# Five zero matmuls, first weights in three loads, and first products in the order of their parts, in a one-core transformer-layer kernel

## The reference, cut to what matters

```python
# x: 1024 tokens x 512; S = 128, F = 1248, G = 6
approx_up = x @ up_w.T                       # 512 -> 128
delta     = x @ gate_w.T - local_point       # 512 -> 128
approx    = approx_up @ local_approx_output.T
for idx in range(G):                         # six powers of delta
    dterm  = exp(log|delta| * (idx + 1) - discount_factor[idx])   # with sign, cut for high powers
    approx = approx + (dterm * approx_up) @ fuse_weight[:, :, idx].T
ffn = (silu(x @ ffn_gate_w.T) * (x @ ffn_up_w.T)) @ ffn_down_w.T
x1  = layernorm(x + approx + ffn)
dq1, dq2, dq3 = nf4_quant_dequant(w1, w2, w3)                     # blocks of 64, hidden width 1376
out = layernorm(x1 + (silu(x1 @ dq1.T) * (x1 @ dq2.T)) @ dq3.T)
```

## Time and profile before

| | |
|---|---|
| median of 3 runs | 418.53 us (418.44 to 418.89) |
| the profiled execution, its own time | 419.06 us |
| its span in the profile | 417.2 us |
| PE busy | 408.3 us |
| DVE, POOL, ACT busy | 314.2, 291.3, 263.9 us |
| DMA share, first 31 us | nearly full; below half in most of the rest |

### The profile page before, as it was taken

One profiled execution on the slowest core, in us unless ns is written; L12 is line 12 of the kernel. 1 busy time (PEld: TensorE's weight loads), 2 busy tenths in 40 slices (PEclk: granted clock), 3 DMA queues, 4 the chain that ended last, 5 costly groups with the idle time before them and its releaser, 6 DMA issues.

```text
span 417.2 us, 5429 instructions
## 1 busy us (share of the span) xinstructions
PE 408.3 (98%) x1820; PEld 334.0 (80%) x1820; DVE 314.2 (75%) x371; ACT 263.9 (63%) x356; POOL 291.3 (70%) x230
## 2 busy tenths in 40 slices
PE   8999999999999999999999999999999999999992
PEld 6888888888878888788888888888888878888882
DVE  3629879879887978999969989898999874115025
ACT  5476676686877547557864976879867864332612
POOL 0078998888995499917992668999989984444330
PEclk9999999999999999999999999999999999999997
DMA  8993110000004342003042000000000000000202
GB/s 267 395 409 131 52 38 26 27 25 25 27 25 126 102 147 101 26 0 103 0 176 97 2 0 1 2 0 0 3 0 0 2 0 2 1 2 1 101 2 101
DMA packets 9355, 26.50 MB, mean 64 GB/s; under 512 B 1296, under 2 KB 1552, under 8 KB 8816
## 3 DMA queue, kind: packets, MB, share of 16 engines
q1 hardware_dynamic: 9328, 26.16, 17.8%
HBM read 24.06 MB, written 2.10 MB: 63 GB/s over the span
## 4 chain that ended last, share of the span: by engine, by line
PE 91%; POOL 2%; DVE 2%; DMA 2%; issue 1%; ACT 0%; SPq 0%; POOLq 0%
PE PS L1178 30%; PE PS L1180 30%; PE PS L1179 30%; DMA h<-xT 2%; POOL l_lo L1133 1%; PE PS L1291 1%; PE PS L1281 1%; POOL level L1103 1%; DVE stats L889 1%; DVE R L884 0%; ACT R L659 0%; DVE x_lo L970 0%; ACT x_hi L573 0%; DVE mv L898 0%; SPq L537 0%
## 5 line engine op out<-in xcount | busy, mean ns | idle before, releaser
L1103 POOL TENSOR_SCALAR level<-side 128x1024 f32<-128x1024 int8 (+2 forms) x119 | 130.0, 1092 | 29.3 <-DVE PS L812 12.1
L1178 PE MATMUL PS<-x_hi,w_hi 128*128 128x512 f32 (+1 forms) x352 | 137.6, 391 | 0.2 <-DVE x_lo L970 0.2
L1180 PE MATMUL PS<-x_hi,w_lo 128*128 128x512 f32 (+1 forms) x352 | 137.1, 390 | 0.0
L1179 PE MATMUL PS<-x_lo,w_hi 128*128 128x512 f32 (+1 forms) x352 | 137.0, 389 | 0.0
L812 DVE TENSOR_TENSOR PS<-PS,level 128x1024 f32<-128x1024 f32 (+2 forms) x102 | 120.3, 1179 | 21.5 <-POOL level L1103 16.8
L573 ACT ACTIVATE side<-Q 128x1024 int8<-128x1024 f32 (+1 forms) x77 | 76.5, 1031 | 18.6 <-DVE PS L808 9.7
L1133 POOL TENSOR_TENSOR l_lo<-h,l_hi 128x512 fp32r<-128x512 f32 (+1 forms) x42 | 58.3, 1396 | 38.5 <-ACT l_hi L573 38.0
L1178 PEld LDWEIGHTS PS<-x_hi,w_hi 128*128 128x128 f32 (+1 forms) x352 | 65.2, 185 | 15.0 <-issue 0.6
L1180 PEld LDWEIGHTS PS<-x_hi,w_lo 128*128 128x128 f32 (+1 forms) x352 | 65.2, 185 | 14.9
L1179 PEld LDWEIGHTS PS<-x_lo,w_hi 128*128 128x128 f32 (+1 forms) x352 | 65.2, 185 | 14.5
L1178 PE MATMUL PS<-x_hi,l_hi 128*128 128x512 f32 x144 | 56.7, 394 | 0.0
(11 more groups left out here) (77 smaller groups left out, 500.4 us busy)
## 6 DMA issues: line engine op xcount, KB each, us to landing
Q<-w SPq DMA_DIRECT2D x10, 512.0 KB, 13.8
raw<-w_in SPq DMA_DIRECT2D x9, 512.0 KB, 11.4
raw<-w_out SPq DMA_DIRECT2D x14, 256.0 KB, 2.6
raw<-w SPq DMA_DIRECT2D x2, 1376.0 KB, 8.4
R<-xN SPq DMA_DIRECT2D x2, 1024.0 KB, 5.4
out<-R SPq DMA_DIRECT2D x8, 256.0 KB, 2.0
raw<-w_fuse SPq DMA_DIRECT2D x7, 256.0 KB, 2.5
h<-xT SPq DMA_DIRECT2D x3, 512.0 KB, 7.1
```

The costliest lines, as they stand in the source:

```text
L1103: g.tensor_scalar(level_of(s), side_of(s), LIMITS[k][1], LIMITS[k][0], ALU.min, ALU.max).then_inc(s_level, 1)
L1178: t_.matmul(dst, a_hi, b_hi, start=start, stop=False)
L1179: t_.matmul(dst, a_hi, b_lo, start=False, stop=False)
L1180: return t_.matmul(dst, a_lo, b_hi, start=False, stop=stop)
```

## The change

`WARM` goes from 8 to 5. The weights of pre are loaded in three parts, for chunk 0, for chunk 1, and for chunks 2 and 3, and ACT and DVE split them in those three parts. Chunk 1 of `x` is loaded in two halves, as chunk 0 was. The two small loads `point` and `discount` become one load of 7 columns, `consts` (made on the host with the discounts repeated for each row), which is issued after job 1 and unit 0; job 1 is now ahead of unit 0. On ACT the exponential of the discounts moves behind the split of job 1. For chunk 0 PE takes the matmuls by the part they need: for a half of the tokens first both products of `w_hi` with `x_hi`, then both of `w_lo` with `x_hi`, then both of `w_hi` with `x_lo`, where each of the latter two groups waits for its own part.

```diff
-WARM = 8
+WARM = 5
...
-            sp.dma_start(w_raw(0)[:, 0:PRE0], w_pre[:, 0:PRE0]).then_inc(s_pre_raw, 16)
-            sp.dma_start(xT_raw[:, 0, 0:HALF], xT[:, 0, 0:HALF]).then_inc(s_x[0], 16)
-            sp.dma_start(xT_raw[:, 0, HALF:TOK], xT[:, 0, HALF:TOK]).then_inc(s_x0b, 16)
-            sp.dma_start(w_raw(0)[:, PRE0:1024], w_pre[:, PRE0:1024]).then_inc(s_raw[0], 16)
-            for c in range(1, DC):
+            for c in range(DC):
+                if c < 2:
+                    part = slice(c * PRE0, (c + 1) * PRE0)
+                    sp.dma_start(w_raw(0)[:, part], w_pre[:, part]).then_inc(s_pre_raw[c], 16)
+                    for a in range(2):
+                        ts = slice(a * HALF, (a + 1) * HALF)
+                        sp.dma_start(xT_raw[:, c, ts], xT[:, c, ts]).then_inc((s_x, s_xb)[a][c], 16)
+                    continue
+                if c == 2:
+                    sp.dma_start(w_raw(0)[:, 2 * PRE0:1024], w_pre[:, 2 * PRE0:1024]).then_inc(s_raw[0], 16)
                 sp.dma_start(xT_raw[:, c, :], xT[:, c, :]).then_inc(s_x[c], 16)
-            sp.dma_start(point_sb[:], point).then_inc(s_point, 16)
-            sp.dma_start(disc[:], discount.broadcast_to([P, G])).then_inc(s_point, 16)
+            load_job(1)
             load_unit(0)
-            load_job(1)
+            sp.dma_start(term_consts[:], consts).then_inc(s_point, 16)
             load_unit(1)
...
             act.wait_ge(s_line0, 1)
-            act.wait_ge(s_point, 32)
-            nc.scalar.activation(fact[:], disc[:], ACT.Exp, scale=-1.0).then_inc(s_fact, 1)
             split_raw(1)
+            act.wait_ge(s_point, 16)
+            nc.scalar.activation(fact[:], disc, ACT.Exp, scale=-1.0).then_inc(s_fact, 1)
             act.wait_ge(s_pre, 2)
...
-            for c in range(DC):
-                if c == 0:
-                    pe.wait_ge(s_pre_hi, 1)
-                    pe.wait_ge(s_pre_lo, 1)
-                elif c == 1:
+
+            pe.wait_ge(s_pre_hi, 1)
+            for half in range(2):
+                xs = slice(half * HALF, (half + 1) * HALF)
+                pe.wait_ge(s_xh, half + 1)
+                for kind in (1, 0):
+                    t_.matmul(PS[:, 2 * kind + half, :], wh0[:, kind, 0, :], x_hi[:, 0, xs], start=True, stop=False)
+                pe.wait_ge(s_pre_lo, 1)
+                for kind in (1, 0):
+                    t_.matmul(PS[:, 2 * kind + half, :], wl0[:, kind, 0, :], x_hi[:, 0, xs], start=False, stop=False)
+                pe.wait_ge(s_xl, half + 1)
+                for kind in (1, 0):
+                    t_.matmul(PS[:, 2 * kind + half, :], wh0[:, kind, 0, :], x_lo[:, 0, xs], start=False, stop=False)
+            for c in range(1, DC):
+                if c == 1:
+                    pe.wait_ge(s_pre_hi, 2)
+                    pe.wait_ge(s_pre_lo, 2)
+                elif c == 2:
                     wait_raw(0)
```

More of the change, by code:

```diff
@@ L256, in job_rows, with build @@
     return P if kind == "fuse" else rows(f, F1) if kind == "out" else rows(f, F2)
-def build(nc, xT, xN, w_pre, w_fuse, w_in, w_out, point, discount, w12, w3, ident_in, out):
+def build(nc, xT, xN, w_pre, w_fuse, w_in, w_out, consts, w12, w3, ident_in, out):
     with ExitStack() as ctx:
@@ L278, in build @@
         ident = sb("ident", [P, P])
-        point_sb, disc, fact = sb("point_sb", [P, 1]), sb("disc", [P, G]), sb("fact", [P, G])
+        term_consts, fact = sb("term_consts", [P, 1 + G]), sb("fact", [P, G])
+        point_sb, disc = term_consts[:, 0:1], term_consts[:, 1:1 + G]
         stats, mv = sb("stats", [P, TT, 6]), sb("mv", [P, TT, 2])
@@ L338, in build @@
         s_zero, s_warm = sem("s_zero"), sem("s_warm")
-        s_pre_raw, s_pre_hi, s_pre_lo = sem("s_pre_raw"), sem("s_pre_hi"), sem("s_pre_lo")
+        s_pre_raw, s_pre_hi, s_pre_lo = [sem(f"s_pre_raw{c}") for c in range(2)], sem("s_pre_hi"), sem("s_pre_lo")
         s_point, s_ident = sem("s_point"), sem("s_ident")
         s_x = [sem(f"s_x{c}") for c in range(DC)]
-        s_x0b = sem("s_x0b")
+        s_xb = [sem(f"s_x{c}b") for c in range(2)]
         s_R = [sem(f"s_R{a}") for a in range(2)]
@@ L958, in _ @@
             hi0, lo0 = raw_parts(0)
-            dve.wait_ge(s_pre_hi, 1)
-            v.tensor_tensor(lo0[:, 0:PRE0], w_raw(0)[:, 0:PRE0], hi0[:, 0:PRE0].bitcast(F32),
-                            ALU.subtract).then_inc(s_pre_lo, 1)
             for c in range(DC):
                 for a in range(2):
-                    if c == 1 and a == 0:
+                    if c < 2 and a == 0:
+                        part = slice(c * PRE0, (c + 1) * PRE0)
+                        dve.wait_ge(s_pre_hi, c + 1)
+                        v.tensor_tensor(lo0[:, part], w_raw(0)[:, part], hi0[:, part].bitcast(F32),
+                                        ALU.subtract).then_inc(s_pre_lo, 1)
+                    elif c == 2 and a == 0:
+                        part = slice(2 * PRE0, 1024)
                         dve.wait_ge(s_whi, 1)
-                        v.tensor_tensor(lo0[:, PRE0:1024], w_raw(0)[:, PRE0:1024], hi0[:, PRE0:1024].bitcast(F32),
+                        v.tensor_tensor(lo0[:, part], w_raw(0)[:, part], hi0[:, part].bitcast(F32),
                                         ALU.subtract).then_inc(s_wlo0, 1)
@@ L977, in _ @@
             beside()
-            dve.wait_ge(s_point, 32)
+            dve.wait_ge(s_point, 16)
             dve.wait_ge(s_pre, 1)
-            v.tensor_scalar(delta, PS[:, 2:4, :], point_sb[:, 0:1], None, ALU.subtract).then_inc(s_delta, 1)
+            v.tensor_scalar(delta, PS[:, 2:4, :], point_sb, None, ALU.subtract).then_inc(s_delta, 1)
             for i in range(2 * C1):
@@ L1312, in _ @@
                     last = product(PS[:, 2 * kind + half, :], wh0[:, kind, c, :], wl0[:, kind, c, :],
-                                   x_hi[:, c, xs], x_lo[:, c, xs], c == 0, c == DC - 1)
+                                   x_hi[:, c, xs], x_lo[:, c, xs], False, c == DC - 1)
                     if c == DC - 1 and half == 1:
@@ L1391 @@
         "w_out": np.ascontiguousarray(a(L0_attn_ffn_down_w).T[:, order]),
-        "point": a(L0_attn_local_point).reshape(S, 1),
-        "discount": a(L0_attn_discount_factor).reshape(1, G),
+        "consts": np.concatenate([a(L0_attn_local_point).reshape(S, 1),
+                                  np.broadcast_to(a(L0_attn_discount_factor).reshape(1, G), (S, G))], axis=1),
         "w12": by_squares(a(L0_ffn_w1), a(L0_ffn_w2)),
```

12 lines of the change are left out of this document (7 added, 5 removed).

## The result

| | before | changed |
|---|---|---|
| median of 19 runs each | 418.67 us (418.25 to 419.35) | 417.87 us (417.59 to 418.53) |
| ratio | | 0.9983, 95% interval 0.9976 to 0.9989 |
| profiled execution, its own time | 419.06 us | 418.42 us |
| its span | 417.2 us | 416.5 us |

417.87 lies inside the predicted range of 416.7 to 418.3, and 0.57 above the predicted 417.3. By the ratio the kernel is faster by 0.7 us (0.5 to 1.0), some 0.6 of the 1.26 us forecast. That is a little under the 0.84 us that I had called the least difference to be told, so it stands at the line between "faster" and "within 0.2%"; with 19 runs on each side the interval does exclude no change.

A forecast was written before the change was run, and what follows sets the result against it. PE bounds the kernel, from when it works without a hole, set by chunk 1's load. 0 (halves) - 1.26 + 0 (loads) + 0 (unit 0) takes 419.06 to 417.80; median 0.53 below, 417.3; range 416.7 to 418.3.

The forecast's parts named there:

- What bounds the kernel, and that the gain lasts: PE works without a hole once chunk 1 has landed; POOL's list moves with PE, so the 1.26 us stays.
- The halves of chunk 1: Chunk 1's first half lands near 7.6, not 8.84; PE starts chunk 1 at 9.12, not 10.38: 1.26 us gained.
- That load keeps its place in bytes and lands at 10.16: Chunk 2's load of `x` lands at 10.16, its products can start at 11.7, and PE wants it at 11.88.
- what is late next: Check of the loads behind chunk 1: chunk 2 has 0.2 us to spare, chunk 3 is ready at 13.4 against 14.6.
- 1.51: Time in us from a chunk's landing, through ACT's `x_hi` and DVE's `x_lo`, to PE's first product of it.
- The sum: Gain of 1.26 us off the profiled 419.06 gives 417.80; the median stands 0.53 below that execution, so 417.3.
- The set-up rival: Each added load pays 1.7 us in the queue; chunk 2 lands at 13.56, 1.9 us slower, 420.5; chance 0.05.
- Five zero matmuls: Before chunk 0 on PE: alone gains nothing; without it chunk 0 ends at 10.03, giving back 0.91 us.
- Order by parts: Chunk 0's second half on PE starts at 7.33 and ends at 8.71, where the old order ends at 9.2.
- Unit 0 and the small loads: Unit 0 lands at 14.14 to 14.60; cost 0 to 0.28 us at the first pair, taken as 0; lateness chance 0.13.
- The clock: PE's pace doubles near 6.3; rival: only after 9.9 the gain is lost, at 12 it is 1 us slower, 419.5; chance 0.03.

The follow-up runs named there:

- the changed kernel, again: The changed kernel run and profiled once more in another session, no edit; 418.08 us, 0.9981 to the kernel before.
- The kernel before, again: The kernel before, unaltered, run and profiled once more as a control; 418.86 us, ratio 1.0003.
- Taking unit 0 out of the way: Changed kernel with the first pair's `w_lo` made on DVE before unit 0's maximum; 418.00 us, 0.9981 to the kernel before.

## Why the prediction held, and where it was wrong

**What bounds the kernel, and that the gain lasts: right.** In all 14 profiles the span ends 403.9 to 404.3 us behind the start of chunk 2. POOL's list moved with PE, as argued: the first POOL row came from 20.91 to

```profile
20.02 2.39 POOL L1132 TENSOR_TENSOR w_lo<-raw,w_hi 128x1024 fp32r<-128x1024 f32 x1 [18.88 <-ACT w_hi L578]
```

and the wait of 0.19 at 168.87 is one of 0.19 at 168.11. No new wait stands behind 20 us.

**The halves of chunk 1: right in kind.** They carry the gain; whole, it falls to 0.9994. The landing was forecast at 7.6 and came at 6.4 (changed), 6.7 (again) and up to 8.4 in others. Counting kilobytes gave the middle of a wide scatter. PE began chunk 1 at 8.98 and 8.42, not 9.12.

**"That load keeps its place in bytes and lands at 10.16": wrong, and the step that failed.** This was said under what is late next, with 0.2 us to spare. Chunk 2 landed at 10.71 and 10.50. I had let the two added loads cost nothing since their bytes are the same. The one of the weights cost nothing that shows (10.03 with chunk 1 whole); the cut of chunk 1 costs chunk 2 between 0.3 and 1.4 us by the extremes of the two groups above, and 0.8 by their means. With 1.51 behind it, 10.71 gives 12.22, PE's start to 0.02, against 11.88 predicted: 0.36 of the gain gone in this profile, 0.15 in the repeat.

**The sum: a late start counted twice.** The median misses the sum before rounding, 417.27, by 0.60. Of that 0.14 is the base, as the median of 3 runs that I started from, 418.53, is 418.67 in 19 runs. The other 0.46 is the gain, 0.80 by medians and not 1.26, and the late chunk 2 is only a part of it. I had counted the gain from 10.38, PE's start on chunk 1 in an execution that was 0.53 above its median. The kernel before, again, was profiled in an execution of 418.71, near its median:

```profile
10.09 0.47 PE L1178 MATMUL PS<-x_hi,w_hi 128*128 128x512 f32 x1 [0.42 <-DVE x_lo L970]
...
12.90 0.39 PE L1178 MATMUL PS<-x_hi,w_hi 128*128 128x512 f32 x1
```

With five zero matmuls alone it is 10.15 and 12.97 (an execution of 418.72), against 10.38 and 13.22. So of the 0.35 us by which 419.06 is longer than 418.71, 0.3 lie in the late start itself, which the change takes away. To count the gain from that start and then to subtract 0.53 for the same late start counts it twice. In executions near their medians chunk 2 starts at 12.94 (the mean of 12.90 and 12.97) with the old loads and at 12.03 in the changed kernel, again. From 1.26 this takes 0.20 at the one end (13.14 against 12.94) and 0.15 at the other (12.03 against 11.88) and leaves 0.91, where 0.80 is measured. The split is an estimate from single executions.

Of the mechanism this is known: it comes with the cut (whole 9.85 to 10.16, cut 10.48 to 11.22); strides in memory are not the cause (10.48 with contiguous halves); larger pieces did not help in the cut by partitions (10.94 with 4 KB pieces); the rate is lower in the microseconds in which the halves pass. At 7 to 8 us it is 389 to 417 GB/s in the four profiles with chunk 1 whole and 197 to 291 in the eight with halves. In the changed kernel the two stretches are

```profile
6.00:7.00 1.00, 1.00 (x4) 0.74 (x3) 1.00 (x3) 0.92 (x3) 0.00 (x0) 1.00 1.18 275
7.00:8.00 1.00, 1.00 (x6) 0.83 (x5) 0.76 (x2) 0.04 (x1) 0.00 (x0) 1.00 0.69 197
```

where the kernel before has

```profile
6.00:7.00 1.00, 1.00 (x5) 0.86 (x4) 0.02 (x1) 0.63 (x1) 0.00 (x0) 1.00 1.02 358
7.00:8.00 1.00, 1.00 (x7) 0.82 (x6) 0.68 (x1) 0.39 (x1) 0.00 (x0) 1.00 1.02 417
```

At 7 to 8 us the DMA share itself is 0.69: here engines stand idle, in the partition-cut kernel they don't. In the seven other profiles with halves it is 0.75 to 0.96, so idle engines are only a part of it.

The packed traces also hold when each of a load's sixteen parts landed. The middle of the sixteen of chunk 2 (between the eighth and the ninth) is at 8.95 to 9.21 with chunk 1 whole and at 9.63 to 9.77 with halves. So most parts are late, by 0.4 to 0.8 us, and not only the last one, which decides. The scatter comes from single parts: in the changed kernel fifteen of the sixteen of chunk 1's second half were there by 7.24, and the last at 8.76. A fixed price for each load does not fit, as the kernel with chunk 2 cut as well, one load more, has the last part of chunk 2 at about 10.7. What in the queue makes the difference stays open.

**The set-up rival: real, but mis-sized.** It had 1.7 us a load and chunk 2 at 13.56; measured are 0.3 to 1.4 us for the cut, under the 1.5 from which it decides. In one form it did win: cut by partitions, where nothing is gained by the first half, the kernel is slower, 1.0020. The Trainium skill, DMA: Bandwidth & Descriptors, "Rules for kernel authors", asks for large transfers: here its direction was right. The 2.0 us that the prediction took from "Anatomy of one DMA" is given there for DMAs that GpSimd issues, and these are issued by SP; paid in line, it would have been far too high.

**Five zero matmuls: right, 0.9 was 0.5.** Alone nothing (1.0000, predicted nothing); with the loads about 0.5 us (0.9994 and 0.9995 against 0.9981 to 0.9983), where I had 0.91 given back. The 0.91 set a chunk 0 that ends at 10.03 against a start of chunk 1 at 9.12. Two things shrink it: the wait for chunk 2 at 12.2, so that only a start of chunk 1 later than about 9.4 (12.2 less twelve matmuls) costs, and PE's pace, which in other executions turned sooner than in the one profile I read. Of the 0.5 itself the two profiles with eight zero matmuls and the new loads show only 0.1 (12.32 against 12.2) and nothing. A turn at 6.0, as in the profile before, would give it: chunk 0 ends at 10.03 by that, chunk 2 starts twelve matmuls later, at 12.8, which is 0.6 behind 12.2. No profile with the new loads caught one, so this is argued and not shown.

**Order by parts: mis-sized, 0.5 us was nothing.** I had the second half of chunk 0 at 6.32, as in all three profiles with the loads of before (6.14 to 6.33). With the new loads it is taken at 4.7 to 5.7 in nine of eleven, though nothing ahead of it in the queue differs; why is open. Its `x_lo` is then ready before PE asks in either order, and what would be left of the 0.5 lies ahead of the wait for chunk 1 or 2.

**Unit 0 and the small loads: the cost right, a reason wrong.** The subtraction ends at 17.63 and PE's first pair follows at 17.78:

```profile
14.84 1.22 DVE L795 TENSOR_REDUCE amax<-Q 128x16 f32<-128x1024 f32 x1 [0.61 <-DMA Q<-w]
...
16.47 1.16 DVE L986 TENSOR_TENSOR w_lo<-raw,w_hi 128x1024 fp32r<-128x1024 f32 x1
```

That matmul starts 0.23 behind the one before it, so no start is lost; its 0.47 instead of 0.39 is at most 0.08. Taking unit 0 out of the way gained nothing. But unit 0 is taken at 14.84, later than the 14.14 to 14.60 I gave it, and the slow microsecond that I had laid to the small loads is not theirs: the kernel before, again, has them with 301 GB/s, and the small load ahead of job 1 costs nothing. I had read a cause out of one stretch of one execution.

**The clock: that rival did not come, but my one turn at 6.3 was one of many.** PE's pace turned near 6.9 in the changed kernel, where the first two matmuls, from 5.47 to 6.49 in PE's timeline above, took 0.5 us each, and the granted-clock column says 1.00 all the while. In the kernel with the small load ahead of job 1 it turned later still, near 7.3: the two matmuls from 7.31 are the first at 0.23 apart. With eight it turned between 4.5 and 6.0, worked out in the last section. With five zero matmuls and the old order, ten passes' loads took

```profile
1.20 3.55 PEld L1308 LDWEIGHTS PS<-level 128*128 128x128 f32 x10 [1.20 <-POOL level L1153]
```

which is nine spacings and one load, 9 x 0.215 + 0.19 = 2.13 at the upper pace alone; the other 1.42 are six to seven passes at the lower pace, and so a turn near 4.1. So with five it lay between 4.1 and 7.3. None came near the 9.9 at which it would have cost the gain. Whether five make a late turn likelier than eight so few profiles can't tell.

## What to carry to other kernels

When a first load is cut so that its first half comes sooner, follow the chain to the load behind it before writing down the gain: with the first wait gone the next one had 0.2 us to spare, and the cut itself cost more than that. Bytes in the order of issue give a fair mean for a landing in a queue's first microseconds, but a single profile gives it only to half a microsecond or a whole one, so take a second profile of the same kernel before a margin under 0.5 us, or a cause for a slow stretch, is believed. Count a gain from an execution near the median: if the profiled one is longer because of the very wait that the change removes, its distance from the median must not be subtracted once more. An edit that is worth nothing alone, such as the fewer zero matmuls, may carry most of the gain of another: try it with and without.

## What the runs showed of the hardware

The moment at which PE's pace doubles moves from one execution to the next. Sixteen passes of the zero matmuls, with PE busy without a hole from 1.20, took these times for their weight loads, in the kernel before again and in the changed one with eight zero matmuls:

```profile
1.20 5.31 PEld L1298 LDWEIGHTS PS<-level 128*128 128x128 f32 x16 [1.20 <-POOL level L1143]
```

```profile
1.20 5.04 PEld L1308 LDWEIGHTS PS<-level 128*128 128x128 f32 x16 [1.20 <-POOL level L1153]
```

In the kernel before they took 5.8: the first product's load is at 7.05. At 0.43 us a pass at the lower level (1.2 GHz) and 0.215 at the upper (2.4 GHz), 16 passes from 1.20 to 7.05 hold 11 at the lower pace, so the turn was at 6.0; to 6.54, where the load of the first product stands in the kernel before again, 9 of them, and the turn at 5.0; to 6.27 in the kernel with eight zero matmuls, 7 to 8 of them, and the turn at 4.5. In the changed kernel it was near 6.9. That is a spread of over 2 us in these four executions with no idle time of PE before it, and chunk 0's end moves with it, by half of that. The Trainium skill, TensorE: Matmul & The Clock Gate, Part 1, says that the moment varies between runs, and the trace agrees.

In the first 10 us cutting a load in two moved the landing of the next one, at the same place in bytes, by 0.3 us or more. And one load's landing scattered by 2 us between executions: the first half of chunk 1, with the same 768 KB ahead of it, was taken by ACT at 6.41 in the changed kernel and at 8.44 in the one with the small load ahead of job 1, which differs only further down the queue.
